# A scanned state-space layer on one core: B and C rows stored twice instead of five times, channels in another order, and two re-ordered steps

## The reference, cut to what matters

```python
h = patches @ W.T + b                                  # (64, 10, 512)
h = h + attn(layernorm(h));  h = h + ffn(layernorm(h))
# attn: rmsnorm -> mamba -> residual -> rmsnorm -> gated MLP -> residual
z, xv, Bm, Cm, dt_in = split(x @ in_proj_w.T)          # 1024, 256, 256, 1024, 128
dt = softplus(dt_in @ dt_proj_w.T + dt_proj_b)         # 1024 channels
dBx = (dt * repeat(xv))[..., None] * repeat(Bm)        # 1024 channels x 16 states
h_t = exp(dt_t * A) * h_{t-1} + dBx_t                  # scan over the 10 steps
y = sum over 16 states of C * h, + D_skip * x, * silu(z);   out = y @ out_proj_w.T
# MLP and ffn: (silu(hn @ gate.T) * (hn @ up.T)) @ down.T, hidden 2048
```

## Time and profile before

| | us |
|---|---|
| median of 3 runs (677.98 to 681.44) | 679.44 |
| the profiled execution | 676.66 |
| its span in the trace | 674.7 |
| TensorE matmul busy | 630.5 |
| VectorE busy | 425.5 |
| GpSimd busy | 428.9 |
| ScalarE busy | 329.3 |

### The profile page before, as it was taken

The page is one execution under the profiler, slowest core; times in us unless marked ns, Lnnn a source line. Parts: engine busy times, 40 slices in busy tenths (PEclk is TensorE's granted clock), DMA queues, the critical chain, the costliest instruction groups (busy, mean ns, idle before and its releaser), DMA issues.

```text
span 674.7 us, 8618 instructions
## 1 busy us (share of the span) xinstructions
PE 630.5 (93%) x2846; PEld 505.2 (75%) x2846; DVE 425.5 (63%) x660; ACT 329.3 (49%) x646; POOL 428.9 (64%) x244
## 2 busy tenths in 40 slices
PE   4959998799999979999979999999999999999998
PEld 3637675466665657777747777766999998999998
DVE  4087997889987859889887988861322223332132
ACT  4358888458887363323346323321642443543441
POOL 0276786348787999887877988644455464445561
PEclk9979999799999979999989999999999999999999
DMA  8799997599999949989866998634443353144421
GB/s 339 253 358 365 316 312 245 169 280 371 336 375 373 362 176 359 412 334 332 316 247 231 345 326 317 200 124 113 140 153 127 124 157 125 63 128 131 147 67 43
DMA packets 49164, 163.50 MB, mean 242 GB/s; under 512 B 4320, under 2 KB 18528, under 8 KB 48480
## 3 DMA queue, kind: packets, MB, share of 16 engines
q1 hardware_dynamic: 49120, 162.95, 69.6%
HBM read 145.24 MB, written 17.69 MB: 242 GB/s over the span
## 4 chain that ended last, share of the span: by engine, by line
PE 73%; DVE 12%; ACT 4%; POOL 4%; issue 3%; DMA 2%; SPq 0%; DVEq 0%; ACTq 0%; POOLq 0%
PE work L990 53%; PE da L990 15%; DVE da L781 7%; PE work L1000 5%; DVE hs L792 3%; POOL hs L453 2%; ACT L528 1%; DMA bb<-b_rows 1%; ACT da L551 1%; DMA c_rows<-c_rows 1%; DMA sm<-small 1%; POOL acc L479 0%; POOL acc L477 0%; POOL hs L466 0%; DVE a L847 0%
## 5 line engine op out<-in xcount | busy, mean ns | idle before, releaser
L781 DVE TENSOR_TENSOR_SCAN da<-da,hs 128x290 f32<-128x290 f32 (+1 forms) x256 | 198.1, 817 | 35.1 <-POOL hs L453 21.2
L453 POOL TENSOR_TENSOR hs<-dtx,bb 128x1160 f32<-128x1160 f32 (+1 forms) x64 | 171.1, 2674 | 59.6 <-PE work L1000 52.4
L551 ACT ACTIVATE da<-dt,a_neg 128x261 f32<-128x261 f32 (+1 forms) x256 | 118.4, 495 | 144.7 <-DVE hs L792 144.5
L432 POOL TENSOR_TENSOR ws<-wraw,ws 128x1024 fp32r<-128x1024 f32 x40 | 101.5, 2538 | 92.8 <-ACT ws L559 92.8
L990 PE MATMUL work<-sq,wraw 128*128 128x290 f32 x512 | 126.0, 407 | 1.5 <-DVE sq L880 1.1
L990 PE MATMUL work<-hn,win 128*128 128x290 f32 (+1 forms) x336 | 103.6, 457 | 17.4 <-DVE hn L855 8.0
L990 PEld LDWEIGHTS work<-sq,wraw 128*128 128x128 f32 x512 | 96.5, 189 | 30.8 <-issue 1.8
L792 DVE TENSOR_TENSOR hs<-da,cb 128x580 f32<-128x580 f32 (+1 forms) x128 | 105.3, 822 | 10.2 <-DMA cb<-c_rows 3.5
L990 PEld LDWEIGHTS work<-hn,win 128*128 128x128 f32 x336 | 65.7, 200 | 51.3 <-issue 26.1
L559 ACT CAST ws<-wraw 128x1024 fp32r<-128x1024 f32 x48 | 50.3, 1048 | 70.6 <-PE da L990 34.4
L990 PE MATMUL work<-hn,ws 128*128 128x350 f32 x480 | 79.2, 323 | 1.6 <-DVE hn L951 1.6
(11 more groups left out here) (97 smaller groups left out, 630.8 us busy)
## 6 DMA issues: line engine op xcount, KB each, us to landing
wraw<-w_stream SPq DMA_DIRECT2D x104, 512.0 KB, 3.8
bb<-b_rows SPq DMA_DIRECT2D x32, 700.0 KB, 6.7
cb<-c_rows SPq DMA_DIRECT2D x32, 700.0 KB, 5.5
bb<-b_rows SPq DMA_DIRECT2D x32, 580.0 KB, 8.2
cb<-c_rows SPq DMA_DIRECT2D x32, 580.0 KB, 6.2
c_rows<-c_rows SPq DMA_DIRECT2D x8, 875.0 KB, 11.0
c_rows<-c_rows SPq DMA_DIRECT2D x8, 725.0 KB, 6.4
win<-w_in SPq DMA_DIRECT2D x4, 1024.0 KB, 13.1
```

The source lines that it names most:

```text
L432: nc.gpsimd.tensor_tensor(ws[:, k % NW, 1, :], wraw[:, split_loads[k] % NRAW, :], ws[:, k % NW, 0, :].bitcast(F32), ALU.subtract).then_inc ...
L453: nc.gpsimd.tensor_tensor(hs[:, u % NH, 0:NQ * n].rearrange("p (n t) -> p n t", t=n), dtx[:, t % 2, 0:n].unsqueeze(1).to_broadcast([P, NQ, ...
L551: last = nc.scalar.activation(dst, src, ACT.Exp, scale=a_neg[:, j:j + 1])
L781: nc.vector.tensor_tensor_scan(da[:, k % ND, 0:w], da[:, k % ND, 0:w], hs[:, u % NH, p * w:(p + 1) * w], 0.0, ALU.mult, ALU.add).then_inc( ...
```

## The change

Rows of B and C are written to DRAM twice instead of five times (`COPIES`). Channels are laid out on partitions in another order (`chan`, `c_row`, `b_row`, `state`, all on the host), so that four neighbouring partitions share a row of C and eight a row of B. A `cb` load reads 32 stretches, each four times; a `bb` load reads 16 stretches, each eight times. Each row of B also stands twice within a copy (`TWICE`), so that one load's 16 stretches are evenly spaced; each half of B is stored by four DMAs instead of one, and each half has a semaphore of its own, which `load_b` waits for at tiles 0 and 4.

In the schedule the second half of B's projection in chunk 0, `in_b` (0, 1), moves from the opening slot to the second one; SP stores it when it comes to unit 1. On ScalarE, a slot whose only `in_z` is one of the seams' is now split in two around the decays, so that in unit 37 `rms2` comes ahead of the decays of unit 38; in unit 50 the first part is `ln2_mean`, in which ScalarE does nothing. After a seam's silu the table with tanh and Exp is loaded instead of the one with Ln and Exp.

```diff
-REPL = P // 8
-COPIES = (REPL + NQ - 1 + NQ - 1) // NQ
+COPIES, TWICE = 2, 2
...
-    slots = [(None, [("bmean", 0), ("tokc", 0), ("mean", 0), ("ln1", 0), ("rms1", 0), ("in_dt", 0), ("in_b", 0, 0), ("in_b", 0, 1),
+    slots = [(None, [("bmean", 0), ("tokc", 0), ("mean", 0), ("ln1", 0), ("rms1", 0), ("in_dt", 0), ("in_b", 0, 0),
                      ("dtp", 0, 0), ("in_c", 0, 0), ("in_x", 0, 0), ("xs", 0, 0)]),
-             (None, [("in_c", 0, 1), ("in_x", 0, 1)])]
+             (None, [("in_c", 0, 1), ("in_b", 0, 1), ("in_x", 0, 1)])]
...
-    b_dram = [nc.dram_tensor(f"b_rows{c}", (COPIES * XB, TS[c]), F32, kind="Internal").ap() for c in range(NCH)]
+    b_dram = [nc.dram_tensor(f"b_rows{c}", (COPIES * TWICE * XB, TS[c]), F32, kind="Internal").ap() for c in range(NCH)]
...
+        def b_in_dram(eng, c, i):
+            eng.wait_ge(b_stored[i], 16 * COPIES * TWICE * (c + 1))
...
-                if u % UNITS == 0:
-                    sp.wait_ge(b_stored, 16 * 2 * (c + 1))
-                rows = b_dram[c].rearrange("(o m n) t -> m o (n t)", m=KI, n=NQ)[m, 2 * q:2 * q + 2 * REPL]
-                src = rows.unsqueeze(1).to_broadcast([2 * REPL, 4, w])
+                if q == 0 and m % 4 == 0:
+                    b_in_dram(sp, c, m // 4)
+                rows = b_dram[c].rearrange("(o m n) t -> m o (n t)", m=KI, n=NQ)[m, 4 * q:4 * q + 16]
+                src = rows.unsqueeze(1).to_broadcast([16, P // 16, w])
...
-                src = c_dram[c][m].rearrange("(o i n) t -> o i (n t)", i=4, n=NQ)[2 * q:2 * q + 2 * REPL]
+                rows = c_dram[c][m].rearrange("(o n) t -> o (n t)", n=NQ)[8 * q:8 * q + 32]
+                src = rows.unsqueeze(1).to_broadcast([32, P // 32, w])
...
-                        sp.dma_start(b_dram[c].rearrange("(k i p) t -> i p k t", p=P, i=2)[i],
-                                     sq[:, 2 + i, 0:TS[c]].unsqueeze(1).to_broadcast([P, COPIES, TS[c]])).then_inc(
-                                         b_stored, 16)
+                        dst = b_dram[c].rearrange("(k y d i r) t -> k d i y r t", k=COPIES, d=TWICE, i=2, r=4 * NQ)
+                        for k in range(COPIES):
+                            for d in range(TWICE):
+                                sp.dma_start(dst[k, d, i], sq[:, 2 + i, 0:TS[c]]).then_inc(b_stored[i], 16)
...
-                    if not parts and not any(s[0] == "in_z" for s in second):
+                    if not parts and not any(s[0] == "in_z" and s not in SEAM for s in second):
                         n = len(second) // 2
                         first, second = second[:n], second[n:]
...
                 if tables[0] == "silu_and_others" and unit is not None:
-                    log_tables()
+                    use_tables("exp_and_others" if any(s in SEAM for s in steps) else "natural_log_exp_and_others")
```

More of the change, by code:

```diff
@@ L260, in build @@
         bb_loaded = [sem(f"bb_loaded{i}") for i in range(NB)]
-        b_stored = sem("b_stored")
+        b_stored = [sem(f"b_stored{i}") for i in range(2)]
         out_stored = sem("out_stored")
@@ L580, in squares @@
                     full(act, ("xs", NCH - 1, KI - 1))
-                    act.wait_ge(b_stored, 16 * 2 * NCH)
+                    b_in_dram(act, NCH - 1, 0)
+                    b_in_dram(act, NCH - 1, 1)
                 elif v < 3:
@@ L602, in step @@
                         full(act, ("xs", c - 1, KI - 1))
-                        act.wait_ge(b_stored, 16 * 2 * c)
+                        b_in_dram(act, c - 1, 0)
+                        b_in_dram(act, c - 1, 1)
                     for k in range(KD):
@@ L1125 @@
     part, ng = np.arange(P), P // NS
-    chan = np.concatenate([m * P + NS * (part % ng) + part // ng for m in range(KI)])
+    chan = np.concatenate([m * P + NS * (part // 4 % ng) + 4 * (part // 32) + part % 4 for m in range(KI)])
     c_row = (np.arange(NQ)[:, None, None] * NQ + NS * np.arange(ng)[:, None] + np.arange(NQ)).reshape(P)
-    b_row = (np.arange(NQ)[:, None, None, None] * NQ + NS * (2 * np.arange(KI)[:, None] + np.arange(2)[:, None, None])
-             + np.arange(NQ)).reshape(XB)
-    state = NQ * ((np.arange(NS) // NQ + part[:, None] // ng) % NQ) + np.arange(NS) % NQ
+    b_row = (np.arange(NQ)[:, None, None, None] * NQ + NS * (2 * np.arange(4)[:, None] + np.arange(2)[:, None, None])
+             + np.arange(NQ)).reshape(P)
+    state = NQ * ((np.arange(NS) // NQ + part[:, None] // 32) % NQ) + np.arange(NS) % NQ
     x = g["x"][:, :, 0]
@@ L1138 @@
     z0, x0, b0, c0, d0 = 0, DI, DI + XB, DI + 2 * XB, 2 * DI + 2 * XB
-    order = [d0 + part, x0 + part, x0 + P + part, b0 + b_row[:P], b0 + b_row[P:]]
+    order = [d0 + part, x0 + part, x0 + P + part, b0 + b_row, b0 + XB // 2 + b_row]
     for m in range(KI):
```

## The result

The changed kernel takes 718.82 us (median; 711.89 to 732.97) beside 678.97 for the kernel before on the same chip. The ratio is 1.0564, interval 1.0522 to 1.0606: slower by 5.6%, where 675.2 us and a range of 671.5 to 681.0 were forecast. (The median holds one run of a slower state, which the ratio leaves out.) The profiled execution took 711.89 us, span 710.0, average granted clock 0.974.

The account below looks back on a forecast made before the run. TensorE was taken to bound the kernel (73% of the span, DMA 2%), with gains only at the start and two seams. -2.9 - 2.6 + 1.3 = -4.2 us on 679.44 gave 675.2 us, range 671.5 to 681.

Parts of the forecast that it names:

- Loads with more repeats: Loads of B and C: reading a DRAM stretch eight or four times costs nothing, priced 0 for both.
- the last one: Rival, chance 0.12: eight-fold reads make DMA the bound of chunk 0, net +6 us, 685.2 us.
- shorter transfers buy nothing: 240 to 340 us, TensorE busy 99.90 of 100 us: claimed no gain there from shorter transfers.
- The second rival: Rival, chance 0.24: B's stores run at half rate, last landing 26.8 us; total 675.9 or 676.9 us.
- Start: Before the first unit: first product 1.7 to 4.1 us earlier by earlier, faster loads; the middle, -2.9 us, taken.
- Half B's 2.03 us: Opening slot: moving B's second half later brings what follows on TensorE 2.03 us earlier, C's store at 24.47.
- the slow bound: B's first four stores at half the full rate: 594 kB take 3.10 us, the last landing at 26.8 us.
- Stores at unit 1: SP's queue: C's store and four B issues ahead of later loads, priced 0, up to 1 us if `load_c(3)` is late.
- First seam: After unit 37: squares ahead of the decays of unit 38 start earlier, -2.6 us.
- full clock: First seam's 8 matmuls: shorter idle time may win up to 1.5 us through TensorE's clock; counted 0.
- Second seam: Before unit 51's squares: an extra table load that nothing covers, +1.3 us, at least 1.0.
- the prediction's own signs of being wrong: Landing of `bb` grows by half, first scan gains under 1.5 us, or the MLP's stretch changes its length.

Follow-up runs that it names:

- e1: Changed kernel, but each load of C's rows reads 128 distinct stretches from the weights in DRAM (C's values wrong): 719.41 us in one timed run.
- e5: Transfers alone, no layer: loads of 128 x 1160 in eight shapes, then stores; four-fold reads 379 GB/s beside 400 for distinct stretches.
- e12: Kernel before with one edit: a bb load reads 16 stretches eight times instead of 32 four times; 747.03 us, ratio 1.1013.
- e13: Changed kernel with bb loads of 128 distinct stretches from the weights (B's values wrong), repeated for an interval: 676.41 us, ratio 0.9977.
- e14: Changed kernel with distinct bb loads from the weights, and half B's projection back in the opening slot: 677.04 us, ratio 0.9977.
- e7: Changed kernel with each row of B four times within a copy, loads 32 x 4, eight stores for each half: 689.77 us, ratio 1.0167.
- e8: Kernel before with ScalarE's part alone: squares ahead of unit 37's decays, tanh table after both seams' silu; 674.97 us, ratio 0.9958.
- e9: Kernel before with ScalarE's part alone, but the tanh table loaded early only after unit 37's silu: 675.34 us, ratio 0.9949.
- e2: Changed kernel, but each load of B's rows reads 128 distinct stretches from the weights (B's values wrong): 671.62 us in one timed run.
- e6: Transfers alone: loads all distinct, into fewer partitions, and DRAM to DRAM; 16 x 8 ran at 230 GB/s distinct, 241 repeated.

## Why the prediction was wrong

**The step that failed** is "Loads with more repeats", with "I take 0 for both". For `cb` that holds (e1, e5: four-fold 379 beside 400 GB/s). For `bb` the eight-fold load runs at 237 instead of 379 GB/s (e5), made DMA the bound and, as the only edit to the kernel before, cost 10% (e12). The rows looked at the earlier trace rows compared four repeats with none and both were fast; they held no load whose outermost dimension was 16, and the working asked how often a stretch is read, not how the write falls on the partitions. "Bytes into SBUF stay" was true and was not enough.

**The rival that came true** is the last one, at 0.12: B's load made DMA the bound. But it did so by its shape and not by repeats, and not where the rival was priced. It had put the point at which DMA becomes the bound at 1.5 times the load time; 379 / 237 is 1.6. It priced 60 to 120 us alone, net +6. There nothing was lost: the changed kernel is 8.2 us behind at unit 6 and 8.3 at unit 16. Chunk 0's 7 us were lost before, while a load of C took 12.46 us. And 240 to 340 us, with a share of 0.88 already and loads of 700 KB, had as little room. The prediction had set that stretch aside as one where "shorter transfers buy nothing"; longer ones cost 33 us from unit 32 on, 17 of them in units 38 to 52, which lie there. How much was not to be had from the rates: in that row 13 loads of B are issued, 13 x 0.72 = 9.3 of 32.3 MB, and at 1.6 times their time the share is 0.88 x (1 + 0.6 x 9.3 / 32.3) = 1.03, just over the brim (an estimate). At the 278 GB/s measured, the 32.3 MB take 116 us (an estimate), which is about the loss; at 237 GB/s for B's loads and 379 for the rest they would take 100. Why the mixture moved more slowly than its parts do by themselves no run shows; everything queued with B's loads landed late.

The second rival, B's stores at half rate (0.24), came true beside it in its mechanism; the next paragraph has the numbers.

**Start, forecast -2.9, bounds -1.7 to -4.1.** In e13 it is -1.1 at unit 0 and -0.8 at unit 8, outside the bounds. Half B's 2.03 us were right for TensorE and C's store, which went out at 24.51 where 24.47 was forecast. That unit 0 gained 2.1 us by it (e13 beside e14) is luck in the number: the reason was the faster landing of its load, not an earlier issue. What failed is the landing of B's stores: the last landed at 28.13, not at 25.35 to 26.8. Four issues took 2.62 us instead of four times 0.41, and the slow bound took half of 383 GB/s where 148 were moved. That the stores use half of the engines is the rule of the Trainium skill cited there (DMA: Bandwidth & Descriptors, section on why a DMA increments its semaphore by 16); the shares of 0.49 here and 0.52 in e5 agree. In the changed kernel itself the start is worse still, +1.6: the stores went out 1.1 us later than in e13 (22.65, 21.53), at a granted clock of 0.87 in 10 to 20 us (1.00 in e13 and before), and the first load of B took 5.43 us instead of e13's 3.81.

**Stores at unit 1, forecast 0 to 1 us.** In the changed kernel C's load behind four issues took 12.46 us and held up the chain; with distinct loads of B (e13) units 0 to 8 lose only 0.3. The price was right for four stores, and it is 4 us for eight (e7).

**First seam, forecast -2.6.** Confirmed: the mean starts 2.7 us earlier in e8, e9, e13 and e14 alike, once the drift up to unit 40 is taken off. Between units 40 and 48 that became -2.9 in e13 and e14, -1.6 in e9 and -4.6 in e8 and e2. For full clock up to 1.5 us more had been named; where it stayed full (e8, e2), 2.0 more came. **Second seam, forecast +1.3.** Confirmed: +1.3 in e8 and +1.7 in e13 and e14, against +0.4 without the load (e9).

With what e13 measured for the three terms the sum is -0.8 - 2.9 + 1.7 = -2.0 us, beside e13's -1.9 in the medians. (The three are read from one execution of e13, so this checks the adding up and not the terms.) The forecast's -4.2 was too much by the start, and the sign was lost to one line that was priced at nothing.

Of the prediction's own signs of being wrong, two came in the changed kernel: the first scan started at 37.25, later than 35.67 instead of earlier, and the MLP's stretch grew. The third came in chunk 1, where the landing of `bb` went from 6.7 to 22.9 us; in chunk 0 it grew from 8.2 to 9.9.

## What to carry to other kernels

Price a changed DMA by its shape on both sides, not by bytes and repeats: look for a row with the same outermost dimension, and where there is none, take a slow end for every stretch in which the DMA share is near 0.9, even where it bounds nothing now. A run of the transfers alone gives the rate. A layout that saves bytes in the stores can cost more in the loads, which are many; here 8.5 MB fewer bytes took 70 us more of the DMA engines' time. One timed execution is not a result where half a per cent matters: the same kernel gave 671.62 us in one and, on another chip, a median of 676.41 in twelve.

## What the runs showed of the hardware that was not expected

- A load into 128 partitions with outermost dimension 16 and 8 inside ran at 230 to 241 GB/s (e5, e6), one of 32 x 4 at 379 to 396, distinct or repeated alike, at a reported DMA share near 1.0 in both. The share can't tell a slow transfer from a full queue; GB/s beside it does.
- DRAM to DRAM the two shapes were equal (320 and 324 GB/s, e6).
- Repeating a DRAM stretch 2, 4 or 32 times cost 8% at most (370, 379 to 396 and 388 beside 400 GB/s, e5).
- A store with 8 outermost ran at a DMA share of 0.49 (changed kernel) to 0.52 (e5) and took SP 0.60 us to issue (median in the changed kernel), against 0.41 with 128 outermost.
